# A two-layer graph network on one core: edges ordered once by source and target bucket, and hops 1 to 4 gathered by one-hot products on TensorE

## The chip, the cores and the metric

The kernel runs on one core of one Trainium2 chip. The metric is the device time of one execution in microseconds (us). Before the change three runs took 6633.33, 6638.75 and 6645.05 us, a median of 6638.75 us.

## The reference, cut to what matters

There are 3125 nodes with 128 features each, and 100000 directed edges (src, dst, weight), sorted by dst. The first layer is an attention network. The part that the change touches is its five hops:

```
e  = einsum(leaky_relu(fh[src] * ft[dst])) * log(deg[dst]) / 16   # 8 heads per edge
a  = softmax of e over the edges of each dst
f  = fe
for _ in range(5):                                  # HOP = 5
    msg = f[src] * a[:, :, None]                    # 8 heads x 16
    agg = segment_sum(msg, dst)
    f   = 0.85 * agg + 0.15 * fe
```

After the hops come a residual, a layer norm and a feed-forward block. The second layer is three graph convolutions, whose edge weights are `edge_weight` normalised by degree; the kernel does these with a dense adjacency matrix that it builds from the edges.

## The kernel before, in words

**Tiling.** The nodes lie in 25 buckets of 125. The edges, sorted by target, are read in tiles of 128; an "item" is one tile seen by one target bucket, so a tile that crosses a bucket's border gives two items. There are 816 items with the padding. Four items make a group (204 groups), and four groups an iteration (51 iterations). The edge of an item lies on the partition. `dloc` holds an edge's target within its bucket, and `ex_it` its eight attention weights (with a factor of 0.85).

**One group of a hop** (`message_groups` on DVE, `sum_groups` on PE). The source rows of four items (128 edges x 128 features each) come into `ga`. DVE makes four one-hot matrices of the targets (`onehots`, L1135) and multiplies the rows by the attention weights (L1192). For each item PE multiplies one-hot by rows in f32 (L878) and adds the result into the accumulator of the item's bucket; the seven banks 0 to 6 of PSUM hold the sums of all 25 buckets. The bucket is a register: `buckets_of` (L448) loads the four bucket numbers of a group from SBUF into registers of PE's sequencer, and each product has its output address worked out from such a register.

**Where the rows come from.** Hop 0 needs no gather: the score stage before it stored each edge's `fe` row in order of edges (`edge_fe`), and SP loads 256 KB per group (L560). In hops 1 to 4 the result of the hop before is written to a table in DRAM (L580). POOL then gathers each item's 128 rows with an indirect DMA (`gather_pass`, L673), 806 per hop, from indices that ACT stages (L736).

**The adjacency matrix.** The second layer's matrix is built on the side, a quarter in each of hops 1 to 4: 352 steps of four "window items". In one step DVE makes a one-hot matrix and four scaled ones (`build_factors`, L1150 and L1154), PE multiplies them (L867, into bank 7), DVE adds the four results in a chain, each needing the last (`build_sums`, L1165), and SP stores four rows of 64 KB (L574). In hops 1 to 4 every second group carries a step until the quarter is done. Hop 1 also sums the edge weights per target (the product L875).

**The other stages.** Before the hops: sorting keys and layer norm, then the score stage (about 215 to 1373 us of the trace). There POOL gathers a double-width row per edge (L673 from `tab_he`), PE turns the target one-hots and gathers the tails (L972, L979), and DVE forms the scores (L1380 to L1389), group by group. Then four scans make the softmax. After the hops: feed-forward, and three convolutions with the stored matrix (L1091).

**Order.** Each engine's program is written out by hand, and semaphores order them. A wait stops that engine's program at its place; what stands behind it is not begun.

Of the kernel before, what the change touches and what calls it, by code (L numbers as in the profile page):

```python
# [12 lines left out]
P = 128  # L13
N_NODES = 3125
N_EDGES = 100000
F = 128
# [28 lines left out]
TABLES = HOPS - 1  # L45
# [6 lines left out]
BUILD_HOPS = HOPS - 1  # L52
KW = -(-WIN_ITEM_COUNT // P)
WIN_ITEMS = KW * P
BUILD_ITERS = WIN_ITEMS // (BUILD_HOPS * BSLOTS * BG)
# [5 lines left out]
assert 1 < FULL_ITERS < BUILD_ITERS < ITERS and SLOTS == 2 * BSLOTS and BG * NB * WN <= BANK  # L61
assert WINDOWS * WN == N_NODES and WPB * WN == BN and BUILD_ITERS * BUILD_HOPS * BSLOTS * BG == WIN_ITEMS
# [4 lines left out]
ROUND = 1.5 * 2.0 ** 23  # L67
PROJ = [(q // 2 * BANKS + q % 2 * BPB, min(NB, q // 2 * BANKS + (BPB if q % 2 == 0 else BANKS))) for q in range(7)]
# [8 lines left out]
MASKS = 9  # L77
# [17 lines left out]
def gnn_stack(nc, a, out):  # L95
    ctx = ExitStack()
    with ctx:
# [12 lines left out]
        tab_f = dram("tab_f", (N_NODES, F))  # L110
# [26 lines left out]
        ex_it = sb("ex_it", [P, ITEMS, HEADS])  # L137
        bucket_row = sb("bucket_row", [1, KB * P], I32)
        stage = sb("stage", [P, SLOTS, G], I32)
        slide = sb("slide", [P, 2 * P - 1], BF16)  # L140
        ident = sb("ident", [P, P])
# [125 lines left out]
        gap_f = gap[:].bitcast(F32)  # L267
        gap_at = [0]
# [13 lines left out]
        ex_flat = ex_it[:].rearrange("p i h -> p (i h)")  # L282
# [22 lines left out]
        prod_ready = sem("prod_ready")  # L305
        cell_sums = sem("cell_sums")
        acc_ready = sem("acc_ready")
        acc_out = [sem(f"acc_out{u}") for u in range(BSLOTS)]
        hops_done = sem("hops_done")
        sum_link = sem("sum_link")  # L310
# [110 lines left out]

        def cut(*at):

            return list(zip(at[:-1], at[1:]))
# [7 lines left out]
        def win_item(s, r, u, j=0):  # L432
            return r * (BSLOTS * BG) + ((s - 1) * BUILD_ITERS * BSLOTS * BG + u * BG + j)

        def steps_before(s):
            return (s - 1) * BUILD_ITERS * BSLOTS


# [5 lines left out]
        WHY_WINDOWS = "a window or a spare row after them"  # L444

# [22 lines left out]
        def _(sp):  # L468
# [45 lines left out]
            sp.dma_start(bucket_row[:], item_bucket_d.rearrange("(a n) -> a n", a=1)).then_inc(bucket_in, 16)  # L514

# [11 lines left out]
            for r0, r1 in cut(0, WIN_OUT_AT, KEY_LOAD_AT, FULL_ITERS, ITERS):  # L527
# [9 lines left out]
                if r0 == KEY_LOAD_AT:  # L537

                    sp.wait_ge(key_out, 16 * steps)
# [17 lines left out]
            with sp.Fori(0, ITERS) as r:  # L557
                for k in range(SLOTS):
                    sp.wait_ge(groups_done, r * SLOTS + (k + 1))
                    sp.dma_start(ga[:, k], edge_fe[:, bass.ds(item_of(r, k), G), :]).then_inc(loaded[k], 16)  # L560
# [3 lines left out]
            for n in range(HOPS):  # L564
                if n:

                    with sp.Fori(0, BUILD_ITERS) as r:
                        for u in range(BSLOTS):
                            _, to = nc.values_load_multi_w_load_instructions(
                                target[0:1, bass.ds(win_item(n, r, u), BG)], engines=(sp.engine,), min_val=0,  # L570
                                max_val=WINDOWS + WIN_SPARE - 1, skip_runtime_bounds_check_because=WHY_WINDOWS)
                            sp.wait_ge(acc_ready, r * BSLOTS + (steps_before(n) + u + 2))
                            for j in range(BG):
                                sp.dma_start(adj[:, bass.ds(to[j], 1), :].rearrange("p w c -> p (w c)"),  # L574
                                             win_acc[:, u, j, :]).then_inc(acc_out[u], 16)
                if n < HOPS - 1:
# [5 lines left out]
            for u in range(BSLOTS):  # L582
                sp.wait_ge(acc_out[u], 16 * BG * (BUILD_HOPS * BUILD_ITERS + 1))
# [263 lines left out]
        def _(pe):  # L847
# [185 lines left out]
            for n in range(HOPS):  # L1033
                if n:
                    pe.wait_ge(sums_out, n * BANKS)
# [600 lines left out]
```

## Time and profile before

| | us |
|---|---|
| median of three runs | 6638.75 |
| the profiled execution's own time | 6636.84 |
| its span, by the profile | 6635.0 |
| busy: PE / DVE / POOL / ACT | 4108.7 / 3545.8 / 3995.5 / 423.6 |

The span is what the profiler saw from the first instruction to the last; 1.8 us of the execution lie outside it. PE is TensorE's products, PEld its weight loads, PEldq its sequencer's own operations; DVE is VectorE, POOL GpSimd, ACT ScalarE, SP the queue that issues most DMAs. A busy share is an average over stages with different limits, so the stages are read one by one. [...]

### The profile page before, as it was taken

The numbers are of one execution on the slowest core, as the hardware profiler recorded it, in microseconds if no ns is written. First come the engines' busy times: TensorE is split into PE (matmuls) and PEld (weight loads), VectorE is DVE, ScalarE is ACT, GpSimd is POOL, SyncE is SP. The second block draws the span as 40 slices with busy tenths as digits, with TensorE's granted clock in tenths as the row PEclk, the third lists the DMA queues.
The fourth block names the chain that finished last, engine by engine and source line by source line (L and its number), as shares of the span: only waits on it lengthen the run. The fifth ranks groups of instructions, "written<-read, shape, count | busy, mean of one in ns | idle before, by whom it ended". The sixth has DMA issues, their size and how long they took to land.

```text
span 6635.0 us, 87679 instructions
## 1 busy us (share of the span) xinstructions
PE 4108.7 (62%) x19868; PEld 3666.2 (55%) x19869; DVE 3545.8 (53%) x7014; ACT 423.6 (6%) x1409; POOL 3995.5 (60%) x4073
## 2 busy tenths in 40 slices
PE   3655645624778888865555544555544555555899
PEld 1444534524668888855545534545443545443899
DVE  7765656677855555435555534555544555544211
ACT  0111111110000000000000000000000000001000
POOL 0577767711047777767777767777776777773000
PEclk9655555557965555555656556565655565656999
DMA  2344464513632222222222212222222222222576
GB/s 58 109 139 146 144 147 135 148 39 117 182 102 77 78 78 77 76 59 77 77 78 77 78 58 76 78 78 77 79 65 68 79 77 78 78 72 76 208 272 231
DMA packets 538438, 671.65 MB, mean 101 GB/s; under 512 B 102388, under 2 KB 423419, under 8 KB 528412
## 3 DMA queue, kind: packets, MB, share of 16 engines
q1 hardware_dynamic: 391970, 345.94, 17.1%
q0 software_dynamic: 143008, 320.73, 16.8%
q10 hardware_dynamic: 3418, 4.48, 0.2%
q8 instruction: 18, 0.29, 0.0%
q14 instruction: 24, 0.20, 0.0%
HBM read 511.17 MB, written 160.80 MB: 101 GB/s over the span
## 4 chain that ended last, share of the span: by engine, by line
POOL 42%; issue 31%; PE 12%; DVE 7%; DMA 6%; SPq 1%; ACT 1%; DVEq 1%; POOLq 0%; ACTq 0%; PEldq 0%; PEld 0%
POOL U L673 42%; PE ps L1091 6%; PE ps L878 3%; DMA U<-edge_fe 2%; DMA U<-tab_f,stage 2%; DVE U L1192 1%; DVE U L1491 1%; DVE U L1463 1%; DVE U L1111 1%; DMA U<-tab_he,stage 1%; PE ps L954 1%; DMA edge_fe<-U 0%; SPq L580 0%; PE ps L867 0%; DMA tab_f<-U 0%
## 5 line engine op out<-in xcount | busy, mean ns | idle before, releaser
L673 POOL DMA_INDIRECT U<-tab_f,stage x3224 | 3102.6, 962 | 1352.6 <-issue 964.1
L878 PE MATMUL ps<-U 128*125 128x128 f32 x8160 | 2051.7, 407 | 1140.3 <-DVE U L1192 1137.4
L878 PEld LDWEIGHTS ps<-U 128*125 128x125 f32 x8160 | 1681.4, 293 | 1282.1 <-issue 1275.9
L1135 DVE TENSOR_TENSOR U<-dloc,iota_p 128x500 f32<-128x500 f32 x1225 | 840.2, 686 | 1974.1 <-DMA U<-tab_f,stage 1919.6
L673 POOL DMA_INDIRECT U<-tab_he,stage x806 | 850.9, 1056 | 438.5 <-issue 246.5
L867 PE MATMUL ps<-gap 128*128 128x125 f32 x2816 | 706.9, 430 | 388.3 <-DVE gap L1165 388.3
L867 PEld LDWEIGHTS ps<-gap 128*128 128x128 f32 x2816 | 630.0, 329 | 460.1 <-issue 460.1
L1192 DVE TENSOR_TENSOR U<-U,ex_it 128x512 f32<-128x512 f32 x1020 | 705.3, 692 | 0.0
L1165 DVE SCALAR_TENSOR_TENSOR gap<-gap,U,ps 128x125 f32<-128x125 f32 x1408 | 483.5, 343 | 154.7 <-DVE gap L1165 79.6
L979 PE MATMUL ps<-U 125*128 x1632 | 422.4, 440 | 210.5 <-ACT U L773 210.5
L875 PEld LDWEIGHTS ps<-w_it,U 128*125 128x125 f32 x1632 | 435.8, 327 | 187.4 <-issue 186.6
L979 PEld LDWEIGHTS ps<-U 125*128 125x128 f32 x1632 | 363.3, 328 | 270.1 <-issue 270.1
L736 ACT COPY stage<-src_it 128x4 int32 (+1 forms) x1023 | 197.6, 193 | 4922.6 <-PE ps L878 4319.9
L875 PE MATMUL ps<-w_it,U 128*125 x1632 | 365.5, 293 | 152.4 <-DVE U L1192 151.9
L972 PE MATMUL ps<-ident,U 128*125 128x128 f32 x816 | 244.1, 454 | 259.1 <-DVE U L1135 258.5
L1154 DVE TENSOR_SCALAR gap<-iota_p,U,raw 128x125 f32<-128x125 f32 x1408 | 389.6, 343 | 0.0
L972 PEld LDWEIGHTS ps<-ident,U 128*125 128x125 f32 x816 | 188.2, 321 | 308.3 <-DVE U L1135 307.3
L1380 DVE TENSOR_TENSOR U<-U,ps 128x512 f32<-128x512 f32 x204 | 140.7, 690 | 378.0 <-DMA U<-tab_he,stage 323.0
L1150 DVE TENSOR_TENSOR gap<-U,iota_p 128x512 f32<-128x512 f32 x352 | 244.2, 694 | 0.2
L1588 DVE TENSOR_TENSOR U<-ps,gap 128x125 f32<-128x125 f32 x75 | 21.7, 289 | 380.9 <-PE ps L1091 380.9
L1091 PE MATMUL ps<-ex_it,U 125*128 125x125 f32 x1500 | 171.5, 274 | 2.3 <-DVE ex_it L1582 2.2
L1091 PE MATMUL ps<-U 125*128 125x125 f32 x1500 | 172.4, 273 | 0.0
(236 smaller groups left out, 2097.1 us busy)
## 6 DMA issues: line engine op xcount, KB each, us to landing
adj<-gap SPq DMA_DIRECT2D x1408, 64.0 KB
edge_fe<-U SPq DMA_DIRECT2D x204, 256.0 KB, 2.5
U<-edge_fe SPq DMA_DIRECT2D x204, 256.0 KB, 2.9
U<-tab_f,stage POOLq DMA_INDIRECT x3224, 2.5
ex_it<-adj SPq DMA_DIRECT2D x30, 1600.0 KB, 6.1
U<-adj SPq DMA_DIRECT2D x30, 1600.0 KB, 6.1
fe_a<-adj SPq DMA_DIRECT2D x15, 1600.0 KB, 6.1
U<-tab_he,stage POOLq DMA_INDIRECT x806, 2.9
```

Source lines behind the costliest of these rows:

```text
L673: pool.indirect_dma_start(to[:, k, j, :], None, table, bass.IndirectOffsetOnAxis(ap=stage[:, k, j:j + 1], axis=0)).then_inc(got[k], 16)
L867: mm = nc.tensor.matmul(ps[:, 7 * BANK + j * CELL:7 * BANK + (j + 1) * CELL], hot_p[:, u, j, :], prod[:, u, j, :], start=True, stop=True)
L875: nc.tensor.matmul(ps[0:BN, bass.ds(b + W_SUMS, 1)], hot[:, k, j, :], w_it[:, bass.ds(r * PER_ITER + (k * G + j), 1)], start=False, stop=F ...
L878: mm = nc.tensor.matmul(ps[0:BN, bass.ds(b * F, F)], hot[:, k, j, :], ga[:, k, j, :], start=False, stop=False, skip_group_check=True)
L972: t = nc.tensor.transpose(bank(k % 2)[0:BN, j * P:(j + 1) * P], hot[:, k, j, :], ident[:])
L979: mm = nc.tensor.matmul(bank(2 + k % 2)[:, j * F:(j + 1) * F], hot_t[:, k % 2, j, :], nb_pad[0:BN, bass.ds(b, 1), :].rearrange("p b f -> p ...
L1091: mm = nc.tensor.matmul(bank(u, BN).rearrange("p (w d) -> p w d", d=WN), rows_[0:BN, b, :], cells[:, :, b, :], start=(b == 0), stop=(b == ...
L1135: return v.tensor_tensor(to[:, (k + ahead) % SLOTS], dloc[:, bass.ds(item_of(r, k, ahead), G)].unsqueeze(2).to_broadcast([P, G, BN]), iota ...
L1150: v.tensor_tensor(hot_p[:, u], win_p[:, bass.ds(i, BG)].unsqueeze(2).to_broadcast([P, BG, P]), iota_p[:].unsqueeze(1).to_broadcast([P, BG, ...
L1154: ins = v.tensor_scalar(prod[:, u, j, :], iota_bn, win_b[:, bass.ds(i, 1)], win_w[:, bass.ds(i, 1)], ALU.is_equal, ALU.mult)
L1165: ins = v.scalar_tensor_tensor(out=win_acc[:, u, j, 0:CELL], in0=before, scalar=win_same[:, bass.ds(win_item(s, r, u, j), 1)], in1=ps[:, 7 ...
L1192: v.tensor_tensor(rows_, rows_, by, ALU.mult).then_inc(msgs_ready, 1)
```

## The change

Hop 0 stays as it was, and so do all results up to the attention weights. What changes:

- **An order by pair of buckets, made once.** In iterations 0 to 24 of the score stage (one per source bucket) DVE and PE count how many edges of that source bucket stand before each edge (`rank_step` on PE, `rank_known` on DVE). The count gives each edge its place (`places`, `pair_items`) in an order by source bucket, and within it by target bucket. In this order an item has one source bucket and one target bucket; there are 1408 items with the padding (352 groups) in place of 816 (204 groups).
- **A scatter.** During hop 0 ACT packs a record of ten numbers per edge (eight weights, source, target), and POOL writes the records to DRAM by indirect DMA at their places, 806 times 128 rows. Then eleven indirect DMAs bring them back in the new order, PE turns them, DVE and ACT keep them.
- **Hops 1 to 4 without DMA gather** (`cell_pass`). The features f of all nodes stay in SBUF as three bf16 parts whose sum is exact (`split_parts`, `split_rest`). For a group, PE multiplies a bf16 one-hot matrix of the sources with each of the three parts, for each of four items, into bank 7 (`gather_items`: twelve products). DVE multiplies bank 7 by the weights (`weigh`), and PE adds up by target as before (four f32 products). The source one-hots are made by DVE from a row of source numbers that SP loads, broadcast over the partitions (256 KB per eight items). PE loads the source buckets and the target buckets of each group into registers.
- **The adjacency steps move.** They stood beside groups of hops 1 to 4. Now 172 of the 352 stand in hop 0, one in each group from iteration 8 on, and the other 180 stand by themselves after hop 0. The sums of edge weights move from hop 1 to hop 0.
- **A late load.** The second load of x, issued before the hops, is issued after them.

The diff, cut to what the time depends on:

```diff
@@ score stage, PE and DVE
+            def rank_step(r):
+                pe.wait_ge(rank_hot, r + (1 - RANK_FROM))
+                for n, m in enumerate((before_m, ones_b)):
+                    for half in range(2):
+                        mm = nc.tensor.matmul(bank(4 + 2 * n + half, HALF), m[:], src_hot[:, half * HALF:(half + 1) * HALF],
+                                              start=True, stop=True)
+                mm.then_inc(rank_sums, 1)
...
+            def rank_known(r):
+                dve.wait_ge(rank_sums, r + (1 - RANK_FROM))
...
+                for n, half in enumerate(halves):
+                    chain(v.scalar_tensor_tensor(out=spare_f[0:NB, half], in0=bank(6 + n, HALF)[0:NB], scalar=1.0,
+                                                 in1=upto[0:NB, half], op0=ALU.mult, op1=ALU.mult,
+                                                 accum_out=cell_n[0:NB, n, bass.ds(r - RANK_FROM, 1)]), False)
+                for n, half in enumerate(halves):
+                    first = run[:, ITEMS - 1:ITEMS] if n == 0 else run[:, HALF - 1:HALF]
+                    chain(v.tensor_tensor_scan(run[:, half], ones[:, 0:1].to_broadcast([P, HALF]), bank(6 + n, HALF),
+                                               first, ALU.mult, ALU.add))
+                for n, half in enumerate(halves):
+                    chain(v.tensor_tensor(here[:, half], bank(4 + n, HALF), run[:, half], ALU.add), n == 1)
+                chain(v.scalar_tensor_tensor(out=here, in0=src_b, scalar=own, in1=here, op0=ALU.is_equal, op1=ALU.mult))
+                chain(v.tensor_tensor(rank, rank, here, ALU.add))
@@ hop 0 on PE and DVE: a step in every group from iteration 8, the rest after it
+                        if r0 >= BUILD_FROM:
+                            build_cells(-BUILD_FROM * SLOTS, r, k)
...
+                        if r0 >= BUILD_FROM:
+                            build_factors(t, r, k)
+                            if k or r0 > BUILD_FROM:
+                                build_sums(t, r, k - 1)
...
+            with dve.Fori(0, BUILD_AFTER // SLOTS) as r:
+                for k in range(SLOTS):
+                    build_factors(STEPS - BUILD_AFTER, r, k)
+                    build_sums(STEPS - BUILD_AFTER, r, k - 1)
@@ POOL: gathers of hops 1 to 4 out, scatter and records in
-            for s in range(1, HOPS):
-                pool.wait_ge(table_out, 16 * (2 + s * BANKS))
-                for r0, r1 in cut(0, FULL_ITERS, ITERS):
-                    gather_pass(staged_before(s), tab_f, ga, r0, r1)
...
+                            pool.indirect_dma_start(
+                                rec_d, bass.IndirectOffsetOnAxis(ap=stage[:, k, j:j + 1], axis=0),
+                                recs[:, k, j, :], None).then_inc(got[k], 16)
@@ hops 1 to 4 on PE
+            def cell_pass(s):
...
+                        for k in range(PSTEPS):
+                            last = r0 and k == PSTEPS - 1
+                            i = r * (PSTEPS * G) + k * G
+                            of = None if last else cell_regs(pe, i + G)
+                            to = cell_regs(pe, i + PITEMS)
+                            pe.wait_ge(weighted, group_of(s, r, k) + 1)
+                            if not last:
+                                if k % 2:
+                                    pe.wait_ge(src_hots, load_of(s, r, (k + 1) // 2) + (1 + PRING))
+                                gather_items((k + 1) % PSTEPS, of)
+                            pe.wait_ge(dst_hots, group_of(s, r, k) + 1)
+                            for j, b in enumerate(to):
+                                mm = nc.tensor.matmul(ps[0:BN, bass.ds(b * F, F)], dst_hot[:, k % PRING, j, :],
+                                                      msg[:, k % PRING, j, :], start=False, stop=False,
+                                                      skip_group_check=True)
+                            mm.then_inc(scattered, 1)
...
+            def gather_items(k, cells):
+                for j, b in enumerate(cells):
+                    for n in range(PARTS_F):
+                        mm = nc.tensor.matmul(bank(7)[:, j * F:(j + 1) * F], src_t[0:BN, k // 2, k % 2 * G + j, :],
+                                              split[0:BN, n, bass.ds(b, 1), :].rearrange("p b f -> p (b f)"),
+                                              start=(n == 0), stop=(n == PARTS_F - 1))
+                mm.then_inc(gathered, 1)
@@ hops 1 to 4 on DVE
+                            if k % 2 == 0 and not (r0 and k == PSTEPS - 2):
+                                compare_sources(s, r, k // 2, 1)
+                            weigh(s, r, k)
+                            if not (r0 and k == PSTEPS - 1):
+                                dst_onehots(s, r, k, 1)
```

## Rows read from the trace of the kernel before

**Rows 1.** The chain of waits of the whole span: shares by engine, by line.
```profile
POOL 42%; issue 31%; PE 12%; DVE 7%; DMA 6%; SPq 1%; ACT 1%; DVEq 1%; POOLq 0%; ACTq 0%; PEldq 0%; PEld 0%
```

**Rows 2.** Busy time by stage: window, length, engines busy (instructions), clock, DMA share, GB/s.
```profile
0.00:1547.00 1547.00, 791.94 (x2969) 625.75 (x2970) 1041.92 (x1483) 209.23 (x470) 870.46 (x838) 0.57 0.41 115
1547.00:1883.00 336.00, 242.06 (x1640) 204.39 (x1641) 281.98 (x420) 0.77 (x4) 22.46 (x11) 0.93 0.58 170
1883.00:2929.00 1046.00, 889.56 (x3975) 852.14 (x3973) 523.72 (x1208) 39.94 (x201) 774.90 (x806) 0.50 0.26 74
2929.00:3975.00 1046.00, 561.49 (x2343) 501.00 (x2344) 523.51 (x1210) 40.40 (x209) 776.66 (x806) 0.56 0.26 74
...
6065.00:6635.00 570.00, 505.51 (x4256) 485.43 (x4256) 126.47 (x280) 55.11 (x121) 0.00 (x0) 0.96 0.59 221
```

**Rows 3.** Who waited for whom in hop 1, 2000 to 2800: total, times, longest.
```profile
DVE U L1135 <- DMA U<-tab_f,stage: 333.3, 158, 4.6
POOL U L673 <- issue: 192.3, 631, 0.3
```

**Rows 4.** Groups by line in hop 1, 2000 to 2800: count, busy us, mean ns, idle before.
```profile
L673 POOL DMA_INDIRECT U<-tab_f,stage x632 | 608.6, 963 | 192.6 <-issue 192.3 <-ACT stage L736 0.3
...
L867 PE MATMUL ps<-gap 128*128 128x125 f32 x624 | 148.9, 417 | 0.0
...
L1192 DVE TENSOR_TENSOR U<-U,ex_it 128x512 f32<-128x512 f32 x159 | 109.0, 686 | 0.0
L1165 DVE SCALAR_TENSOR_TENSOR gap<-gap,U,ps 128x125 f32<-128x125 f32 x316 | 108.5, 343 | 34.8 <-DVE gap L1165 17.8
L1135 DVE TENSOR_TENSOR U<-dloc,iota_p 128x500 f32<-128x500 f32 x159 | 108.3, 681 | 333.6 <-DMA U<-tab_f,stage 333.3 <-DVE gap L1165 0.2
L1154 DVE TENSOR_SCALAR gap<-iota_p,U,raw 128x125 f32<-128x125 f32 x312 | 86.4, 342 | 0.0
L1150 DVE TENSOR_TENSOR gap<-U,iota_p 128x512 f32<-128x512 f32 x78 | 54.4, 697 | 0.0
```

**Rows 5.** Groups by line in hop 0, 1600 to 1860.
```profile
L878 PE MATMUL ps<-U 128*125 128x128 f32 x1439 | 206.1, 285 | 54.6 <-DVE U L1192 52.1 <-issue 0.7
...
L1135 DVE TENSOR_TENSOR U<-dloc,iota_p 128x500 f32<-128x500 f32 x181 | 124.3, 687 | 30.5 <-DMA U<-edge_fe 25.4
```

**Rows 6.** PE sequencer, one hop-0 group: min/median/max ns, first to last start us.
```profile
L878 PEldq FUSED_REGOPS  x4: 46/46/46, 1702.5 to 1702.8; - x4
L448 PEldq FUSED_REGOPS  x1: 46/46/46, 1703.0 to 1703.0; - x1
L448 PEldq TENSOR_LOAD <-bucket_row x1: 331/331/331, 1703.1 to 1703.1; - x1
L872 PEldq ALU_OP  x1: 32/32/32, 1703.5 to 1703.5; - x1
```

**Rows 7.** The same for the four products of one score group (operand by register).
```profile
L979 PEldq FUSED_REGOPS  x4: 55/55/55, 726.8 to 727.2; - x4
```

**Rows 8.** Score stage, groups by line, 250 to 1350.
```profile
L673 POOL DMA_INDIRECT U<-tab_he,stage x761 | 803.5, 1056 | 282.2 <-issue 233.2 <-ACT stage L736 49.0
L979 PE MATMUL ps<-U 125*128 x1543 | 399.3, 440 | 200.1 <-ACT U L773 200.1
...
L1430 DVE SCALAR_TENSOR_TENSOR U<-U 128x1408 f32<-128x1408 f32 x1 | 1.6, 1624 | 0.1
```

**Rows 9.** Two groups of DVE there in order of time: start us, us.
```profile
721.19 0.69 DVE L1380 TENSOR_TENSOR U<-U,ps 128x512 f32<-128x512 f32 x1 [0.77 <-PE ps L979]
...
725.01 0.69 DVE L1380 TENSOR_TENSOR U<-U,ps 128x512 f32<-128x512 f32 x1 [0.26 <-PE ps L979]
```

**Rows 10.** The softmax's scans, 1430 to 1520.
```profile
L1463 DVE TENSOR_TENSOR_SCAN U<-U,ex_it 128x6528 f32<-128x6528 f32 x1 | 13.8, 13758 | 0.0
```

**Rows 11.** The turn from hop 1 to hop 2, in order of time.
```profile
2925.20 3.88 DVE L1534 TENSOR_TENSOR U<-ps,fe_a 125x512 f32<-125x512 f32 x7
2929.13 3.16 PE L851 MATMUL ps<-zeros 1*128 1x512 bf16 x7 [4.19 <-DVE U L1534]
```

More of the change, by code:

```diff
@@ L76 @@
 W_SUMS = (NB + 1) * F
-MASKS = 9
+MASKS = 12
+PAIRS = NB * NB
+PAIR_ITEM_COUNT = N_EDGES // P + PAIRS
+PK = -(-PAIR_ITEM_COUNT // P)
+PITEMS = PK * P
+PGROUPS = PITEMS // G
+PSTEPS = 8
+PITERS = PGROUPS // PSTEPS
+PRING = 4
+LOAD = 2 * G
+PLOADS = PITEMS // LOAD
+PARTS_F = 3
+REC = HEADS + 2
+DUMP = TILES * P
+RANK_FROM = 0
+ENDS_AT, PAIRS_AT = 28, 29
+assert PRING == SLOTS and PITERS * PSTEPS == PGROUPS and PSTEPS == 2 * PRING and PLOADS == PITERS * PRING
+HALF = ITEMS // 2
+assert ITEMS % 2 == 0 and HALF <= BANK
 assert PER_ITER == CHUNKS and ITEMS % CHUNKS == 0 and CHUNKS * HEADS == P and NB * BN == N_NODES
@@ new lines, in _ @@
+            with sp.Fori(0, BUILD_FROM + 1) as r:
+                for k in range(SLOTS):
+                    load_group(r, k)
+            sp.wait_ge(targets_ready, 1)
+            first = -(BUILD_FROM + 1) * SLOTS
+            with sp.Fori(BUILD_FROM + 1, ITERS) as r:
+                for k in range(SLOTS):
+                    load_group(r, k)
+                    store_step(first, r, k)
+            sp.wait_ge(cell_out, 16 * 2)
+            sp.dma_start(cell_row, cell_d.rearrange("(a n) -> a n", a=1)).then_inc(cell_in, 16)
@@ new lines, in _, with split_parts @@
+            act.wait_ge(var_ready, 4)
+            nc.scalar.activation(dinv[0:BN], dinv[0:BN], ACT.Sqrt).then_inc(std_ready, 1)
+            def split_parts(n):
+                for k in range(BANKS):
+                    b0, b1 = bank_buckets(k)
+                    act.wait_ge(sums_out, n * BANKS + k + 1)
+                    nc.scalar.copy(split[0:BN, 0, b0:b1], na[0:BN, b0:b1]).then_inc(split_high, 1)
+                for k in range(BANKS):
+                    b0, b1 = bank_buckets(k)
+                    act.wait_ge(split_link, n * BANKS + k + 1)
+                    nc.scalar.copy(split[0:BN, 1, b0:b1], rest[0:BN, k, 0:(b1 - b0) * F].rearrange(
+                        "p (b f) -> p b f", f=F)).then_inc(split_mid, 1)
@@ new lines, in _ @@
+            act.wait_ge(built, 1)
+            for k in range(PK):
+                act.wait_ge(rec_turned, k + 1)
+                at_ = slice(k * P, (k + 1) * P)
+                banks = [3 * (k % 2) + n for n in range(3)]
+                nc.scalar.copy(ex_it[:, at_, HALF_HEADS:], bank(banks[1]).rearrange("p (h i) -> p i h", i=P)
+                               ).then_inc(rec_kept_a, 1)
+                nc.scalar.copy(dst_c[:, at_], bank(banks[2], P)).then_inc(rec_kept_a, 1)
+            for s in range(HOPS - 1):
+                split_parts(s)
@@ new lines, in keep_records, with chain @@
+            def keep_records(k):
+                dve.wait_ge(rec_turned, k + 1)
+                v.tensor_copy(ex_it[:, k * P:(k + 1) * P, 0:HALF_HEADS], bank(3 * (k % 2)).rearrange(
+                    "p (h i) -> p i h", i=P)).then_inc(rec_kept_v, 1)
+            RANK_LINKS = 8
+            def rank_known(r):
+                dve.wait_ge(rank_sums, r + (1 - RANK_FROM))
+                links_ = [0]
+                def chain(ins, wait=True):
+                    links_[0] += 1
+                    ins.then_inc(rank_link, 1)
+                    if wait:
+                        dve.wait_ge(rank_link, r * RANK_LINKS + (links_[0] - RANK_FROM * RANK_LINKS))
+                own = iota_p[:, bass.ds(r + (1 - RANK_FROM), 1)]
+                halves = [slice(half * HALF, (half + 1) * HALF) for half in range(2)]
+                for n, half in enumerate(halves):
[10 more added lines that the diff above has]
+                chain(v.tensor_tensor(rank, rank, here, ALU.add))
+                assert links_[0] == RANK_LINKS
```

531 lines of the change are left out of this document (410 added, 121 removed).

## The prediction

> **What bounds the kernel now.** I read the chain of waits first: POOL holds 42% of it [rows 1]. The busy times by stage say where: hops 1 to 4 take 1046 us each, 4182 of 6635 us, and the third and fourth look like the second [rows 2]. In a hop POOL issues 806 gathers; DVE waits for their rows (333 us of 800), POOL for nothing but its own issue [rows 3]. One gather costs 0.963 us and 0.305 us of issue [rows 4], 1.27 in all, so a group of four takes 5.1 us; 204 of them make the hop. PE and DVE lie below that pace, and so the adjacency steps cost nothing in hops 1 to 4: DVE is busy for 524 of 1046 us. Hop 0 shows the same group without a gather: 181 groups in 260 us, 1.44 us each, at 0.93 of the full clock over the stage [rows 2, 5].
>
> The change takes the gather away and puts four things in its place: products on PE in hops 1 to 4, the adjacency steps in the open, a round trip of records, and a count in the score stage.
>
> **Hops 1 to 4, per group (now 352 a hop).** Four chains run at once; the longest sets the pace.
>
> *PE's sequencer.* A product whose address comes from a register needs an operation of the sequencer first. In a score group the four such operations start 0.13 us apart [rows 7], and the four products of a hop-0 group take from 1702.5 to 1703.0, 0.12 us each [rows 6]. I take 0.13 for the gather, which has the same form (a moving table row named by a register), and count one operation per product: each has another address, as the three parts lie apart. Twelve products: 1.6 us. Four scatter products: 0.5. One load of four registers takes from 1703.0 to 1703.5, 0.5 us with its own operation [rows 6]; two per group: 1.0. The waits (weighted, one-hots, and the sources in every second group) need an ALU operation each, 32 ns and a gap, some 0.1 [rows 6], 0.25 in all. All this stands in one program in order: **3.35 us**. In hop 0 the same work is 1.1 us of 1.44 and hides under DVE; here nothing is long enough to cover it.
>
> *The loop over bank 7.* The next gather may not write the bank before DVE has weighed it. Gather 1.6, the tail of its last product 0.29 [rows 5], weighing 0.69 (form of L1192 [rows 4]), two signals of 0.15 (the step between dependent L1165s, 17.8 us in 117 times in the same window [rows 3, 4], as an estimate for two engines): 2.9 us.
>
> *PE's array.* An f32 product is two records of 0.143 us in hop 0 (206.1 us for 1439 [rows 5]) and of 0.239 at half clock (148.9 for 624 [rows 4]). A bf16 product is one pass, at most half a record's: 0.07 or 0.12. Eight records and twelve passes: 2.0 us at full clock, 3.35 at half. So the granted clock, 0.93 in hop 0 and 0.50 to 0.56 in the others [rows 2], which I can't foretell, changes little.
>
> *DVE.* Weighing 0.69, one-hots 0.69, half a source comparison (no row of this shape; between nothing and 1.2 us for 1024 elements at L1430's rate [rows 8], I take 0.4): 1.6 us. SP's load for two groups is 256 KB in 6.7 us, against the 170 GB/s of hop 0 [rows 2]; it hides.
>
> Bounds of a group: 1.6 (DVE alone) and 3.9 (register loads that don't overlap the weighing); I take 3.35, because every term of it has a row. Between hops: the sums out 3.88 us [rows 11]; the split into three parts, two DVE passes of that size, 7.8; lags between ACT and DVE, clearing and the first gather, some 6: 18 us. A hop is 352 x 3.35 + 18 = 1197 us, four are 4789, before 4182: **+607**.
>
> [...]
>
> **Hop 0 and the adjacency steps.** DVE per step: factors (54.4 + 86.4)/78 = 1.81 us, sums (108.5 + 34.8)/79 = 1.81; messages (108.3 + 109.0)/159 = 1.37 [rows 4]. A group with a step is 4.99 us of DVE. For PE at half clock, hop 1 is an upper bound: 889.6 us less 88 steps of 1.91 (148.9/78) leaves 3.54 per group [rows 2, 4], with the step 5.45. I take 5.1: 172 groups are 877 us. The 32 groups before need 79 (by 1600 us some 14 are done, the rest at 1.44), the end 13. Hop 0 becomes 969 us instead of 336: **+633**. SP has five transfers a group here, 512 KB in 5.1 us, 100 GB/s, below what hop 0 moved. POOL's scatter runs beside it: 806 x 1.27 = 1020 us from 1600, over before the next part is; if the steps were quicker it would show.
>
> Behind hop 0, 180 steps stand alone. PE's product waits for the sums of the step before, as bank 7 is single: sums 1.81, product 1.91, signals 0.3 give 4.1 us with the factors hidden under the product; bounds 3.6 (DVE alone) and 5.5 (nothing overlaps). **+738**. In hops 1 to 4 before, POOL's pace covered all of this; the cover is gone.
>
> **Records.** Eleven rounds of nine turns, 18 records of 0.239, are 47 us; with the gathers, copies, the store of source numbers and the first load I take **+68** (47 to 110).
>
> **Score stage.** Per iteration DVE adds three operations on 816 elements (0.94 each at L1430's rate [rows 8]), two scans of 408 (0.86 at 2.11 ns [rows 10]), four of 408 (0.47) and six dependent steps of 0.15: 7.3 us. POOL paces the stage at 1.056 + 0.31 = 1.36 per gather [rows 8], 21.9 per iteration; DVE and PE, when not waiting, need 3.8 per group [rows 9], so 15.3 + 7.3 = 22.6, and PE's four products may add 1.4 to the way. That is 0.7 to 2.1 over POOL, 18 to 53 us in 25 iterations. The lumps (thirteen operations at the start, some forty in the end) are half hidden: **+70**; bounds 0 and 260 (nothing hidden).
>
> **Tail.** The late load of x covers itself but for some 5 us: **+5**.
>
> Sum: 607 + 633 + 738 + 68 + 70 + 5 = +2121 on the profiled execution's own 6636.84 (its span is 6635.0): **8758 us**. That execution lies 1.9 us (0.03%) below the median of the runs. About 0.2% is what a measurement of this kernel can tell from no change.
>
> **Rivals.**
> - *A, the forecast* (0.70): 8450 to 9100 by the bounds of its terms; 0.1 us per group is 141 us over the 1408 groups, 0.1 us per adjacency step 35.
> - *B, one register operation per item* (0.15): the three parts share an address. Sequencer 0.5 + 0.5 + 1.0 + 0.25 = 2.3 us, the loop the same; 8758 - 1408 x 1.05 = 7280. For it: the register is the same three times. Against: neighbouring products of hop 1 and hop 0 show an operation each.
> - *C, the sequencer runs ahead and hides* (0.05): the loop remains with a gather at the array's pace, 0.86 + 0.29 + 0.69 + 0.3 = 2.1 us; 7000. Against: the register loads stand behind the scatter and before the wait.
> - *D, faster* (0.05): the array is the bound, at the pace of the convolutions (505.5 us for 4256 records, 0.119 [rows 2]): 8 x 0.119 + 12 x 0.06 = 1.67 us, with registers and weighing beneath. 8758 - 1408 x 1.68 = 6390. It decides from 1.84 us per group down: there the hops give back the 1514 us that the rest costs. Against: bank 7 is single, so weighing lies between two gathers.
> - *E, slower still* (0.05): the register loads don't overlap the weighing, 2.9 + 1.0 = 3.9 us; 9530.
>
> **How the numbers follow.** The time is A's. A and B hold 0.85; B's error and C's reach down to 7000, A's up to 9100, so 7000 to 9100 leaves out D, E and the outer part of A, under 0.2. Within A alone I would say 8450 to 9100. Faster is D (0.05); 0.01 of what lies between C and D falls within 0.2%; slower 0.94.
>
> **What would show it.** Per-group pace of hops 1 to 4: 3.3 us, with PE idle and waiting on its own issue, not on DVE; sequencer operations twelve per gather, 0.13 apart. If PE waits on the weighing with 2.1 to 2.9 us a group, B or C. Hop 0 near 970 us with DVE busy over 90%; a stretch of about 740 us behind it with neither POOL nor messages. Score stage 0 to 100 us longer. The prediction is wrong if a group takes under 2.9 us, or if the steps outside the hops cost less than 1200 us together.

## The result and the profile after the change

The changed kernel takes 8703.75 us (median of four runs, 8700.06 to 8707.32), the kernel before 6636.91 us on the same chip: a ratio of 1.3112, 95% interval 1.3089 to 1.3135. The forecast was 8758 us, in a range of 7000 to 9100. The profiled execution has a span of 8702.4 us, 2067 us more than before.

The busy time by stage, as in [rows 2]: from to, length, PE, PEld, DVE, ACT and POOL busy (instructions), granted clock (1.00 is full clock), DMA share, GB/s. The stages are all up to hop 0, hop 0, the lone adjacency steps, the records, hops 1 to 4 (hop 3, which is like hop 2, is left out), the rest.

```profile
0.00:1625.00 1625.00, 775.76 (x3073) 611.95 (x3074) 1239.73 (x1821) 208.74 (x470) 864.85 (x843) 0.59 0.40 110
1625.00:2613.00 988.00, 983.54 (x4634) 981.33 (x4635) 794.30 (x1956) 90.57 (x720) 767.92 (x717) 0.50 0.39 105
2613.00:3386.00 773.00, 370.82 (x1459) 324.16 (x1460) 562.56 (x1632) 14.03 (x98) 103.53 (x103) 0.50 0.22 63
3386.00:3434.00 48.00, 25.22 (x103) 18.97 (x101) 21.91 (x52) 14.91 (x36) 8.43 (x9) 0.61 0.45 148
3434.00:4590.00 1156.00, 955.51 (x7040) 743.53 (x7040) 520.18 (x881) 0.00 (x0) 0.00 (x0) 1.00 0.10 39
4590.00:5757.00 1167.00, 957.55 (x7045) 744.08 (x7046) 531.70 (x901) 7.63 (x14) 0.00 (x0) 0.99 0.10 39
...
6925.00:8093.00 1168.00, 959.49 (x7046) 745.07 (x7047) 531.61 (x901) 7.63 (x14) 0.00 (x0) 0.99 0.10 38
8093.00:8702.00 609.00, 508.68 (x4260) 486.61 (x4258) 130.56 (x287) 55.38 (x121) 0.00 (x0) 0.93 0.57 210
```

Set against the forecast's terms:

| stage | before | after | difference | forecast |
|---|---|---|---|---|
| up to hop 0 | 1547 | 1625 | +78 | +70 |
| hop 0 | 336 | 988 | +652 | +633 |
| lone steps | 0 | 773 | +773 | +738 |
| records | 0 | 48 | +48 | +68 |
| hops 1 to 4 | 4182 | 4659 | +477 | +607 |
| rest | 570 | 609 | +39 | +5 |
| sum | 6635 | 8702 | +2067 | +2121 |

A hop now has 352 groups. One group of hop 2, first in order of time (start, us, operation, idle before it and who ended it), then PE's own operations in it (minimum, median and maximum in ns, first and last start):

```profile
5000.41 1.65 PE L1112 MATMUL ps<-U 125*128 x12 [0.88 <-issue]
...
5001.95 1.14 PE L1103 MATMUL ps<-U 128*125 128x128 f32 x8
5002.21 0.69 DVE L1472 TENSOR_TENSOR U<-ps,ex_it 128x512 f32<-128x512 f32 x1 [2.19 <-PE ps L1112]
5002.82 0.67 DVE L1462 TENSOR_TENSOR U<-raw,iota_p 128x500 f32<-128x500 f32 x1
...
5003.67 1.53 PEld L1112 LDWEIGHTS ps<-U 125*128 125x128 bf16 x12 [0.77 <-issue]
```

```profile
L1112 PEldq FUSED_REGOPS  x12: 46/46/60, 5000.3 to 5001.7; - x12
...
L1103 PEldq FUSED_REGOPS  x4: 46/46/46, 5001.8 to 5002.3; - x4
...
L553 PEldq TENSOR_LOAD <-U x3: 330/332/335, 4999.8 to 5003.0; - x3
```

The weighing (L1472) ends at 5002.90, but the next gather (L1112) begins only at 5003.67: in between PE's sequencer finishes the second register load (0.33 us from 5002.98) and two operations for the waits. Twelve register operations take from 5000.3 to 5001.8, 0.126 us each. Over a longer stretch of the hop, 4800 to 5600, nobody holds PE up but its own issue, as the forecast said (before, by [rows 3], DVE waited for the transfer and POOL for its issue). Columns: engine and line, whom it waited for, us in total, times, longest:

```profile
DVE U L1472 <- PE ps L1112: 440.8, 244, 2.2
PEld ps L1112 <- issue: 185.5, 244, 1.1
PE ps L1112 <- issue: 140.2, 244, 0.9
```

Hop 0 with its steps, 1800 to 2500, by line (count, busy us, mean ns, idle before). The lines of PE and its weight loads have no idle time at all; DVE has a little (L1425, 87 us of 700).

```profile
L1065 PE MATMUL ps<-U 128*125 128x128 f32 x1102 | 424.1, 488 | 0.0
L1062 PEld LDWEIGHTS ps<-w_it,U 128*125 128x125 f32 x1100 | 299.5, 332 | 0.0
...
L1049 PE MATMUL ps<-gap 128*128 128x125 f32 x1102 | 262.9, 417 | 0.0
...
L1425 DVE SCALAR_TENSOR_TENSOR gap<-gap,U,ps 128x125 f32<-128x125 f32 x550 | 190.3, 346 | 87.1 <-DVE gap L1425 25.6 <-PE ps L1049 18.3
```

One lone step in order of time: the sums (L1425), then at once the product (L1049), whose result the next sums await. And the rest of the kernel: the load of x behind the hops, and DVE's wait for it.

```profile
3000.15 1.33 DVE L1425 SCALAR_TENSOR_TENSOR gap<-gap,U,ps 128x125 f32<-128x125 f32 x3 [0.15 <-DVE gap L1425]
...
3001.63 2.04 PE L1049 MATMUL ps<-gap 128*128 128x125 f32 x8 [2.21 <-DVE gap L1425]
...
3003.82 0.35 DVE L1425 SCALAR_TENSOR_TENSOR gap<-gap,U,ps 128x125 f32<-128x125 f32 x1 [0.48 <-PE ps L1049]
...
8097.38 0.56 ACTq L1008 DMA_DIRECT2D U<-in_x  x1
...
8132.97 2.29 DVE L1385 TENSOR_REDUCE stat<-U 125x16 f32<-125x2048 f32 x1 [32.04 <-DMA U<-in_x]
```

In the score stage, 300 to 1340, DVE waits less for gathered rows and POOL more for ACT's indices, which wait for DVE. The first line is of the kernel before, the other two of the kernel after:

```profile
DVE U L1380 <- DMA U<-tab_he,stage: 298.9, 146, 15.7
```

```profile
POOL U L821 <- ACT stage L900: 120.3, 18, 48.4
DVE U L1817 <- DMA U<-tab_he,stage: 115.2, 45, 21.0
```

### The profile page after: what moved, and what is told of

It reads as the page before. It is cut to its first block, busy times and chain, and to the rows that moved or that the text cites. A ratio compares the mean times of both kernels' runs of the same rounds, so it can differ in the third digit from the quotient of the medians.

```text
span 8702.4 us, 162184 instructions
## 1 busy us (share of the span) xinstructions
PE 6495.1 (75%) x41703; PEld 5400.2 (62%) x41704; DVE 4864.4 (56%) x9329; ACT 406.5 (5%) x1487; POOL 1744.7 (20%) x1671
## 4 chain that ended last, share of the span: by engine, by line
PE 67%; issue 14%; DVE 11%; POOL 3%; DMA 2%; DVEq 1%; ACT 1%; SPq 1%; POOLq 0%; ACTq 0%; PEldq 0%; PEld 0%
PE ps L1112 27%; PE ps L1103 17%; PE ps L1049 7%; PE ps L1065 6%; PE ps L1358 5%; POOL U L821 3%; DVE gap L1425 3%; PE ps L1062 2%; PE ps L1227 1%; PE ps L1220 1%; DVE U L1933 1%; DVE U L1905 1%; DMA U<-tab_he,stage 1%; DVE gap L1413 1%; DVE gap L1541 1%
## 5 line engine op out<-in xcount | busy, mean ns | idle before, releaser
L1112 PE MATMUL ps<-U 125*128 x16896 | 2354.7, 228 | 821.0 <-issue 792.5
L1112 PEld LDWEIGHTS ps<-U 125*128 125x128 bf16 x16896 | 1628.5, 96 | 1626.0 <-issue 1085.6
L1472 DVE TENSOR_TENSOR U<-ps,ex_it 128x512 f32<-128x512 f32 x1408 | 976.5, 694 | 2538.2 <-PE ps L1112 2538.2
L1103 PE MATMUL ps<-U 128*125 128x128 f32 x11264 | 1608.4, 284 | 0.0
L1103 PEld LDWEIGHTS ps<-U 128*125 128x125 f32 x11264 | 1346.6, 187 | 45.1 <-issue 0.2
L1049 PE MATMUL ps<-gap 128*128 128x125 f32 x2816 | 695.2, 425 | 402.2 <-DVE gap L1425 402.2
L1462 DVE TENSOR_TENSOR U<-raw,iota_p 128x500 f32<-128x500 f32 x1408 | 944.4, 671 | 0.0
L1049 PEld LDWEIGHTS ps<-gap 128*128 128x128 f32 x2816 | 635.1, 330 | 448.8 <-issue 448.8
L869 POOL DMA_INDIRECT rec_d<-ex_it,stage x806 | 847.4, 1051 | 245.5 <-issue 228.8
L1425 DVE SCALAR_TENSOR_TENSOR gap<-gap,U,ps 128x125 f32<-128x125 f32 x1408 | 487.2, 346 | 273.8 <-PE ps L1049 100.4
L1065 PE MATMUL ps<-U 128*125 128x128 f32 x1632 | 628.1, 489 | 0.0
L1227 PE MATMUL ps<-U 125*128 x1632 | 402.4, 424 | 217.3 <-ACT U L930 216.4
L1062 PEld LDWEIGHTS ps<-w_it,U 128*125 128x125 f32 x1632 | 444.5, 333 | 5.8 <-issue 5.8
L1065 PEld LDWEIGHTS ps<-U 128*125 128x125 f32 x1632 | 443.1, 332 | 0.0
L1062 PE MATMUL ps<-w_it,U 128*125 x1632 | 344.3, 280 | 4.2 <-DVE U L1449 4.2
L1455 DVE TENSOR_SCALAR U<-gap,pidx 125x1024 bf16<-125x1024 bf16 x704 | 339.1, 482 | 0.1
L1402 DVE TENSOR_TENSOR U<-dloc,iota_p 128x500 f32<-128x500 f32 x409 | 282.5, 691 | 86.1 <-DMA U<-edge_fe 53.4
```

The costliest lines, as they stand in the source:

```text
L869: pool.indirect_dma_start(rec_d, bass.IndirectOffsetOnAxis(ap=stage[:, k, j:j + 1], axis=0), recs[:, k, j, :], None).then_inc(got[k], 16)
L1049: mm = nc.tensor.matmul(cells_at(j), hot_p[:, k % BSLOTS, j, :], prod[:, k % BSLOTS, j, :], start=True, stop=True)
L1062: nc.tensor.matmul(ps[0:BN, bass.ds(b + W_SUMS, 1)], hot[:, k, j, :], w_it[:, bass.ds(r * PER_ITER + (k * G + j), 1)], start=False, stop=F ...
L1065: mm = nc.tensor.matmul(ps[0:BN, bass.ds(b * F, F)], hot[:, k, j, :], ga[:, k, j, :], start=False, stop=False, skip_group_check=True)
L1103: mm = nc.tensor.matmul(ps[0:BN, bass.ds(b * F, F)], dst_hot[:, k % PRING, j, :], msg[:, k % PRING, j, :], start=False, stop=False, skip_g ...
L1112: mm = nc.tensor.matmul(bank(7)[:, j * F:(j + 1) * F], src_t[0:BN, k // 2, k % 2 * G + j, :], split[0:BN, n, bass.ds(b, 1), :].rearrange(" ...
```

## The experiments

The theory: in hops 1 to 4 PE's sequencer, in program order, sets the pace; in hop 0 and behind it the adjacency steps cost what they need, as no gather covers them. The rivals are the array, the loop over bank 7, and DVE. The experiments ran on chips on which the kernel before took 6685 to 6720 us. Where their stages ahead of the hops are the same, they agree with the changed kernel's within 12 us, so gains are read from the stages. Each ratio is to the kernel before on the same chip. "Per group" is the time from the first weighing of hop 1 to the last of hop 4 over 1408: 3.31 us in the changed kernel.

**1. Fixed addresses.**

```diff
-  split[0:BN, n, bass.ds(b, 1), :]
+  split[0:BN, n, bass.ds(b, 1) if n == 0 else slice(j, j + 1), :]
```

> Of the twelve products of a group's gather the first part of each item keeps its address from a register, and the second and third parts are read at a fixed address (bucket j in place of the item's bucket, so the gathered numbers are wrong from the 2nd bf16 part on). Eight register operations per group go; the products, loads, waits, and all of DVE stay. Theory 1 (PE's sequencer in program order sets the 3.34 us of a group): the eight products then follow at the array's or the weight load's own pace, which the traces so far do not show; between 0.06 and 0.10 us instead of 0.126, so a group falls by 0.2 to 0.55 us, 1408 groups by 280 to 770 us: 7930 to 8420 us. Theory 2 (the array or the weight loads of 125x128 set the pace at 0.125 us a product, and the register operations only ride along): no change, 8690 to 8715 us. Theory 3 (the loop over bank 7 with the weighing in it sets the pace): the gather is part of that loop and shortens by the same amount if the products do, but PE would then be seen waiting for the weighing, not for its own issue.

Measured: 7278.07 us, 1.0829 of before (1.0798 to 1.0861); 2.29 us a group. The gather of one group:

```profile
L1112 PEld LDWEIGHTS ps<-U x12: 96/98/99, 4002.6 to 4003.2; 125*128 125x128 bf16 x12
...
L1112 PEldq FUSED_REGOPS  x4: 55/58/60, 4002.5 to 4002.9; - x4
```

The same twelve products begin within 0.58 us instead of 1.42, those at fixed addresses 0.056 us apart. So the array can do them more than twice as fast, and theory 2 falls. Theory 3 wants PE to wait for the weighing; from 3500 to 4300 it still waits above all for its own issue:

```profile
PE ps L1112 <- issue: 132.4, 299, 0.6
PE ps L1112 <- DVE U L1472: 34.5, 43, 1.1
```

The gain, 1.02 us a group, is twice what I expected. I had left out that products at fixed addresses queue up, and that the sequencer's next operations (those of the scatter, from 4003.0 on) then run while the array still works (its last gather record begins at 4003.2).

**2. One register load.**

```diff
-  of = None if last else cell_regs(pe, i + G)     # 4 registers
-  to = cell_regs(pe, i + PITEMS)                  # 4 registers
+  both = cell_regs(pe, r * (PSTEPS * 2 * G) + k * 2 * G)   # 8, side by side in cell_row
+  of, to = both[:G], both[G:]
```

> Nothing is left out: the source buckets of group g+1 and the target buckets of group g lie side by side, and one load brings eight registers where two loads brought four each. The products and their register operations stay. Theory 1 (sequencer): one load with its own operation is 0.50 us of a group; if eight registers take as long as four the group falls from 3.34 to 2.85, to 8000 us; if eight take twice the 0.33 us, only the operation and a gap of 0.17 go, to 8465 us. I expect 8000 to 8465. Theory 2 (array or weight loads) and theory 3 (loop over bank 7, 2.7 to 2.9 us by the trace: 1.5 gather, 0.4 to the weighing, 0.7 weighing, 0.1 to 0.2 back): 2 gives no change; 3 stops the fall at 2.7 to 2.9 us, with PE waiting for DVE, at 7810 us at the least.

Measured: 8382.23 us, 1.2472 of before (1.2436 to 1.2508); 3.08 us a group, 0.23 less. The load of eight:

```profile
L553 PEldq TENSOR_LOAD <-U x263: 587/590/594, 3499.4 to 4297.5; - x132
```

Eight registers take 0.59 us where four take 0.33: what is saved is one operation and its gaps. Two loads with their operations hold the sequencer for 0.99 us in the changed kernel, the one load with its operation for 0.76 here: that is the 0.23 us by which the group got shorter. If the array or the loop over bank 7 set the pace, it would have stayed.

**3 and 4. An f32 gather, alone and with one load.**

```diff
-  for n in range(PARTS_F): ... src_t (bf16) x split[0:BN, n, b]    # 12 products
+  ... src_t (f32) x na[0:BN, b]                                    # 4 products, no split
```

> One f32 product per item gathers straight from the f32 features: four products with an address from a register in place of twelve, source one-hots in f32, no split into three parts between the hops. Theory 1 (sequencer): eight operations of 0.126 go, 3.34 to 2.33 us a group, then the loads of 1.0 us are the largest term; minus 1.01 x 1408 = 1420 us and 4 x 8 us of split: 7250 us; between 7100 and 7500, as f32 one-hots cost DVE up to 0.3 us a group more beside it. Theory 2 (array): eight f32 records of 0.119 to 0.143 in place of twelve passes at 0.125 leave 0.95 to 1.14 us in place of 1.5: minus 0.36 to 0.55 us a group, 7900 to 8200 us; if a bf16 pass is really 0.06 us in the array, a f32 gather is longer, not shorter, and the time stays or rises.

> The f32 gather and the single load of eight registers together; nothing is left out. Theory 1 (sequencer): 2.33 us less 0.17 to 0.5 would be 1.85 to 2.15, but the loop over bank 7 (1.14 gather, 0.1, 0.69 weighing, 0.1 to 0.2) is 2.05 to 2.15, DVE 1.7 to 2.0, and sixteen f32 records 1.9 to 2.3: about 2.15 us a group, 7000 us (6850 to 7150), and the waits of PE are then for DVE or none. Theory 2 (array): the load hides, so the time is that of the f32 gather alone, within 30 us.

Measured: 7271.31 us, 1.0819 (1.0788 to 1.0851), and 7212.71 us, 1.0732 (1.0701 to 1.0763); 2.28 and 2.24 us a group. The array does more work now (eight f32 records, 0.111 us apart, 0.97 us of weight loads a gather; the twelve of experiment 1 took 0.67), and the hops are 31% shorter than in the changed kernel. Already with the f32 gather alone PE is seen to wait for the weighing (3500 to 4300):

```profile
PE ps L1089 <- DVE U L1449: 66.8, 244, 1.1
```

What the prediction and this expectation took for the array and for f32 one-hots stands in the traces:

- A bf16 product is one record (from 4000 to 4800 in the changed kernel, 2881 of L1112 beside 240 weighings of twelve products each), an f32 product two (2800 of L1089 beside 350 weighings of four, in experiment 3).
- At full clock (0.99 from 4000 to 4800) bf16 records begin 0.056 us apart in experiment 1 and f32 records 0.111 here. At half clock (0.50 from 436 to 438 in the changed kernel) the bf16 products of 408 columns begin 0.34 us apart (L1209, the first at 436.28, the third at 436.96), 0.107 per 128 columns; f32 records begin 0.213 apart (L867 in the kernel before, eight in 1.91 us, the last of them 0.42 long, from 2400.73 on). So a bf16 record takes half of an f32 record at either clock: 0.056 and 0.107 us, where the prediction had 0.07 and 0.12, and the condition in the expectation (0.06) is met. The gather did not get shorter in the array: 0.97 us of weight loads against 0.67.
- The comparison of sources for two groups takes DVE 0.746 us in f32 (L1432 here) and 0.482 in bf16 (L1455 in the changed kernel): 0.13 us a group more, of the 0.3 allowed for.

With both edits the loop over bank 7 is the bound: gather, weighing, next gather, 2.26 us around (4001.45 to 4003.71). PE's own products lie close beneath it: PE is busy for 2883 of the 3160 us of these hops.

```profile
4001.45 1.15 PE L1092 MATMUL ps<-U 125*128 x8 [0.28 <-DVE U L1452]
...
4002.76 0.69 DVE L1452 TENSOR_TENSOR U<-ps,ex_it 128x512 f32<-128x512 f32 x1 [0.93 <-PE ps L1092]
...
4003.71 0.48 PE L1092 MATMUL ps<-U 125*128 x2 [0.22 <-DVE U L1452]
```

The expectation for the fourth was 7000 us: the loop is 0.1 us longer than I had it, and the third was already close to it, so the single load gave 59 us.

**5. Steps out of hop 0** (`BUILD_FROM = 49` in place of 8).

> The adjacency steps of hop 0 but eight are moved into the stretch behind it, so that 344 in place of 180 stand alone there; nothing is left out. Alone a step took 4.29 us in the changed kernel (773 us for 180), so the stretch should take 1476 us, 703 more. What hop 0 gives back tells what its steps cost. Theory 1 (the prediction's: DVE sets hop 0's pace, 5 us a group with a step and 1.4 without): hop 0 falls from 988 to about 350 us, total 8770. Theory 2 (TensorE sets it, at half clock, with 24 f32 records of 0.21 us a group: 8 of the step, 8 of the weight sums, 8 of the messages): 164 groups lose a third of 5.09 us, hop 0 becomes about 710 us, total 9130. Theory 3 (as 2, but without the steps the granted clock rises to the 0.93 of hop 0 before): 16 records of 0.11 are 1.8 us a group, hop 0 about 400 us, total 8820.

Measured: 9120.12 us, 1.3642 (1.3615 to 1.3669). Hop 0 and the lone stretch:

```profile
1624.00:2331.00 707.00, 702.52 (x3312) 700.88 (x3311) 300.89 (x478) 63.90 (x512) 551.07 (x510) 0.50 0.35 84
2331.00:3798.00 1467.00, 703.74 (x2765) 614.66 (x2763) 1070.06 (x3106) 40.47 (x306) 309.36 (x310) 0.50 0.22 63
```

Hop 0 falls to 707 us and not to 350: theory 2. PE is busy for 702.5 of them at a clock of 0.50, without the steps too. A step costs 1.7 us in hop 0 (281 us for 164) and 4.26 alone.

**6. Two banks, and x early.**

```diff
-  return ps[:, 7 * BANK + j * CELL: ...]
+  return ps[:, (6 + k % 2) * BANK + j * CELL: ...]     # lone steps only
-  pe.wait_ge(acc_ready, ... (t + k + 1))
+  pe.wait_ge(acc_ready, ... (t + k + 1 - two))         # the sums of the step before last; two: lone steps only
...
+  act.dma_start(x_sb[1:BN], nodes_of(a["x"])[1:BN])    # before hop 1
-  act.dma_start(x_sb[0:BN], nodes_of(a["x"]))          # after the hops
+  act.dma_start(x_sb[0:1], nodes_of(a["x"])[0:1])
```

> Two edits in two stretches, nothing left out. (a) Of the 180 steps that stand alone the even ones put their four products into bank 6, the odd ones into bank 7, so the next product no longer waits for the sums of the one before. Theory 1 (the loop product, sums, product through the single bank sets 4.29 us): the step falls to what DVE needs, 1.81 factors, 1.83 sums and signals, 3.7 us: minus 0.5 to 0.6 x 180, 90 to 110 us. Theory 2 (DVE itself or the stores set it): under 20 us. (b) The load of x for 124 of the 125 partitions is issued before hop 1; only the first partition, where the bucket numbers lie, is loaded behind the hops. The wait for x behind the hops was 35.5 us (32 of it idle); it should fall under 6: minus 30 us, if the transfer is what is waited for; if the queue's own latency is, it stays. Together 8560 to 8590 us.

Measured: 8579.72 us, 1.2837 (1.2816 to 1.2859). The lone stretch, and the wait for x:

```profile
2608.00:3283.00 675.00, 376.52 (x1462) 324.89 (x1461) 546.09 (x1631) 14.04 (x98) 102.76 (x103) 0.50 0.25 72
```

```profile
8006.63 2.29 DVE L1387 TENSOR_REDUCE stat<-U 125x16 f32<-125x2048 f32 x1 [4.72 <-DMA U<-in_x]
```

Both as expected: 98 us of the lone stretch were the loop through the single bank, and 27 of 32 us of idle time were the transfer of x, which begins together with three loads of 1600 KB.

**7. No weight sums in hop 0** (the product L1062 is left out).

> The sums of edge weights per target are left out of hop 0 (four of its twelve products a group), so the degrees of the convolutions are wrong. Theory 1 (DVE sets hop 0's pace at 5 us a group, as the prediction has it): under 20 us less. Theory 2 (TensorE at half clock sets it: 24 records in 5.09 us, 0.212 each): with 16 records TensorE needs 3.4 us, and DVE's 4.2 busy and 0.15 to 0.4 of signals are next: 4.3 to 4.6 us a group, minus 85 to 135 us in 172 groups and some 30 in the 32 groups before: 8540 to 8620 us.

Measured: 8614.94 us, 1.2888 (1.2866 to 1.2909). Hop 0, and who waits in it from 1800 to 2500:

```profile
1624.00:2519.00 895.00, 591.85 (x3004) 528.76 (x3003) 777.65 (x1955) 80.09 (x640) 699.69 (x639) 0.71 0.45 115
```

```profile
PE ps L1049 <- DVE gap L1422: 214.9, 146, 2.2
```

Hop 0 is 93 us shorter, and now PE waits for DVE. The 172 groups with a step take 822 us, 4.78 each in place of 5.07; the rest is in the 32 groups ahead of them, 73 us in place of 113. The granted clock is 0.71 and not 0.50, so fewer products and a higher clock can't be told apart here; both are TensorE's. So TensorE set the pace, but DVE lies only 0.3 us a group beneath it.

**8. The cover given back.** In the kernel of experiment 4, with x early, 176 of the 180 lone steps are put into hops 1 to 4.

```diff
+  if k % 4 == 1: build_half(s, r, k // 4)     # PE: two products into free columns of bank 6
...
+  if k % 4 == 1: half_factors(s, r, k // 4)   # DVE
+  if k % 4 == 2: sum_half(s, r, k // 4)
```

> The f32 gather with one load of eight registers and the early load of x, and beside it 176 of the 180 lone adjacency steps go back into hops 1 to 4, as half steps of two window items, one in every fourth group; their products lie in the free columns of bank 6, and the scatter behind them waits for DVE's sums. Nothing is left out. The lone stretch should shrink from 773 to some 20 us and the wait for x from 35 to under 6: 7213 less 785 is 6430 us, if the half steps cost nothing in the hops. DVE was busy 1.73 us of 2.2 a group there; the steps add 3.64 x 176 / 1408 = 0.46 us, so 2.19. Theory 1 (the loop over bank 7 sets the hops and DVE has slack in it): 0.05 to 0.25 us a group more, 6500 to 6780 us. Theory 2 (DVE's work in front of a weighing lies on the loop): all of 640 us come back, 7070 us. The kernel before is at about 6640 to 6720 us.

Measured: 6898.57 us, 1.0313 (1.0296 to 1.0330). The half steps' products begin anew in bank 6, beside the sums of the last target bucket, and these sums come out wrong. The hops:

```profile
2803.00:6322.00 3519.00, 3127.08 (x23946) 2795.75 (x23946) 2753.98 (x5299) 0.00 (x0) 0.00 (x0) 1.00 0.19 64
```

A group takes 2.50 us, 0.26 more than in experiment 4: some 360 us for 176 steps, 2.05 each, against 4.29 alone. Of the 785 us that go, 360 come back in the hops and some 110 in a new wait: the lone steps end at 2639 us, but POOL's scatter ends at 2741, and the records wait for it.

**9 and 10. What can be had.** Nine joins the edits of 4 and 6. Ten is 8 with the products adding onto columns that DVE clears, 28 more steps alone, and the comparison of sources behind a weighing.

> The edits that gained, together, with the adjacency steps where the change put them: f32 gather, one load of eight registers, two banks for the lone steps, early load of x; nothing is left out. They lie in different stretches, so they should add: 7213 less 98 (lone steps) and 32 (x) is 7083 us, 7060 to 7110. Slower than the kernel before (6640 to 6720) by some 6%.

> The kernel with the steps back in the hops (6899 us), mended and trimmed; nothing is left out. There a half step's products began anew (start) in bank 6, beside the sums of the last bucket, and the output differed where those sums go; here they add onto columns that DVE clears after each half step. If that is the cause, the output is the reference's; that is what this run settles first. Trims: 28 more steps stand alone, in the 132 us in which the scatter on POOL is not done yet (minus 57 us, as a step in the hops cost 2.05 us: 360 / 176), and the comparison of sources no longer stands in front of a weighing (minus up to 120 us by the trace, where a weighing came 0.45 us late once in four groups). The clearing costs 0.3 us of DVE once in four groups, some on the path: plus 0 to 120. Theory 1 (the loop over bank 7 with DVE's late weighing sets the hops): 6720 to 6850 us, near the kernel before but not under it. Theory 2 (TensorE's own work, 8.9 of 9.96 us in four groups, sets them): 6830 to 6960.

Measured: 7081.68 us, 1.0585 (1.0567 to 1.0604), as expected to 2 us; and 7014.98 us, 1.0487 (1.0469 to 1.0506), outside what either theory gave. In ten the sums of the last bucket are right again. The half steps' sums were moved ahead of the target one-hots, and DVE is seen waiting for the product, PE for the clearing, itself 0.267 us (3600 to 4400, 76 half steps):

```profile
PE ps L1148 <- DVE U L1536: 83.6, 186, 1.1
...
DVE item_cols L1488 <- PE ps L1141: 51.4, 76, 0.7
PE ps L1130 <- DVE ps L1496: 51.1, 76, 0.7
```

That is 0.7 us a half step on each side. The hops take 3618 us, 99 more than in eight, though 28 steps fewer stand in them. Which of the three edits in the hops (the clearing, the earlier sums, the later comparison) cost how much was not tested apart. No version that was run is faster than the kernel before.

## Why the prediction was right, step by step

- **PE's sequencer sets the group in hops 1 to 4: right, and shown.** Forecast 3.35 us, measured 3.28 within a hop (hop 2 takes 1167.5 us from sums to sums, some 13.6 of them between the hops). Taking operations out (1, 3) or one load out (2) shortens the group; more array work (3) does not lengthen it. The sign set for it came, PE waiting for its own issue and not for DVE, and neither sign of being wrong did (3.28 us a group, 1590 us outside the hops). The array's terms held as well: one record to a bf16 product, half as long as each of an f32 product's two (experiment 3). The sequencer's terms were 0.13 (0.126 measured) and 0.5 for a load (0.498 from load to load). Rivals B and C fall by the twelve operations and by the wait for issue, D by the 2.26 us at which the loop stops even the f32 gather, E because the loads run beside the weighing. The 130 us too many are 0.07 us in 1408 groups (101 us), 4.4 us at each turn of a hop (18) and hop 1, 11 us shorter than the others, as the sums out and the split ahead of it lie in earlier windows.
- **Hop 0, 969 us forecast, 988 measured: the size right, the engine not.** I named DVE, with over 90% busy; it was 80%, and PE 99.5% at a clock of 0.50. The step that failed is that PE at half clock was only taken as an upper bound (5.45 us a group with a step), and not at all for the 32 groups ahead of the steps. These were put at the 1.44 us that hop 0 had before, at a clock of 0.93 and without weight sums; they took 113 us in place of 79, at a clock of 0.50. What I left without a price of its own are the weight sums: a product of one column still loads its weights anew, 0.33 us a load, as many loads as the messages have. Experiments 5 and 7 show it. With weight sums and eight steps hop 0 takes 707 us, 3.47 a group, close to the 3.54 that I had worked out for PE at half clock in hop 1; with steps and no weight sums 895; with both 988; before, with neither, 336. So a large part of the +652, which I gave to the steps, is the weight sums, and the two do not add up, because PE sets the pace with them and DVE without. (Hop 0 with neither, but beside the scatter, was not run.) That the number came out is luck: DVE's need (4.78) and PE's (5.07) are nearly the same.
- **The scatter, forecast to be over with hop 0: wrong, at no cost here.** It began at 1652 us and ended at 2745, 132 us into the lone steps, which cover it. In experiment 8 they no longer do.
- **The lone steps, 738 forecast, 773 measured: right.** The loop of sums and product through one bank was named; it is 4.29 us and not 4.1 (the terms written down, 1.81, 1.91 and 0.3, sum to 4.02), and experiment 6 gives 98 us back when the bank is doubled.
- **That the cover of POOL's pace is gone: right.** A step costs 4.3 us alone, 1.7 in hop 0, 2.05 in faster hops (experiments 5 and 8). It was never free, only covered.
- **Score stage, +70 forecast, +78 measured: the size right, the place not.** DVE's wait for gathers fell by 184 us in 300 to 1340, and the count's operations stand there now. From the first group's scores to those of the 101st, the stretch of the count, 59 us were added, where 18 to 53 were forecast. The operations behind the last group, which were taken as half hidden, added nothing: from its scores to the first message of hop 0 it is 178 us before and after. The two errors cancel in part. No experiment took the count apart, so this one rests on the traces.
- **Records, 68 forecast, 48 measured**: I took a turn for two records of PE, 198 in all and 47 us; it is one, 99 in all, and PE is busy for 25 us of the stage. The 48 also hold 8 us of the split ahead of hop 1.
- **The late load of x, +5 forecast, +39 measured: wrong.** I had it cover itself but for 5 us, without a price for the transfer. It is issued at the same time as three adjacency buckets of 1600 KB, and 35.6 us pass until the operation that waits for it starts, 32 of them idle; issued before the hops, 4.7 are left (experiment 6). Another 4.5 of the 39 are only the cut between the stages, which before the change lies behind the sums of the last hop and after it ahead of them.

The errors, +19, +35, +8 and +34 against -130 and -20, sum to -54 us: the total is nearer than its largest terms, because the errors cancel in part.

## What to carry to other kernels

When operands get their addresses from registers, price PE by its sequencer: here 0.126 us for each product that needs an address of its own, against 0.056 us between bf16 products at fixed ones, and 0.33 us for a load of four registers, 0.59 for one of eight. Fewer, heavier products (four f32 in place of twelve bf16) were then worth 1.0 us a group, though the array had more to do. And before a slow engine's stage is made faster, list what hides under it, and price each piece where it will stand afterwards: here the stages into which the pieces were moved grew by 652 and 773 us.

## What the runs showed of the hardware that was not expected

- The sequencer runs ahead: with eight of twelve products at fixed addresses, the operations for the following products overlap the products still queued, and 0.127 us was saved for each operation removed, as much as a product with such an operation takes.
- A load of registers grows with their number: 0.332 us for four, 0.590 us for eight.
- TensorE's granted clock was 0.50 over hop 0 while PE was busy for 983.5 of 988 us, and 0.71 when the products of one column were left out and it was busy for 591.9 of 895. In the hops it was 0.99 to 1.00 at 82% busy. So a high busy share was no sign of full clock here; why hop 0 stays at the lower level was not settled.
- A gather in f32 ran at 0.111 us a record at full clock, with no gap from the four register operations: beside two records to a product they are hidden (four operations from 4002.2 to 4002.6 in experiment 3, eight weight loads from 4002.30 to 4003.27).
